# The routing of each mixture's first block moved into the stage ahead of it

## The reference

```
xn     = layernorm(x)
p      = softmax(xn @ router_W + router_b)        # 15 experts
cw     = p where p is among the 3 largest, else 0
x     += shared(xn) + sum over e of cw[e] * (relu(xn @ eW1[e] + eb1[e]) @ eW2[e] + eb2[e])
```

## Time and profile before

| | us |
|---|---|
| time, median of 3 runs | 2176.91 |
| lowest and highest | 2173.97, 2182.21 |
| the profiled execution's own time | 2175.81 |
| its span in the trace | 2174.1 |
| mean granted TensorE clock, as a share of full | 0.939 |

### The profile page before, as it was taken

How to read it: one execution, slowest core, us unless ns; L and a number is a source line. 1 busy time by engine, 2 the same in 40 slices (tenths; PEclk the granted TensorE clock), 3 DMA queues, 4 the chain that set the end, 5 groups by cost and what they waited for, 6 DMA issues and landing times. The chain is left out here.

```text
span 2174.1 us, 31063 instructions
## 1 busy us (share of the span) xinstructions
PE 1862.9 (86%) x9650; PEld 1279.9 (59%) x9650; DVE 1684.7 (77%) x4191; ACT 1200.8 (55%) x2004; POOL 903.4 (42%) x881
## 2 busy tenths in 40 slices
PE   6786699998899967674699978999999999988998
PEld 4564577777677723332577755555555555546777
DVE  6996788866788779998788867766766767738886
ACT  3442266653566634443466644665666666556666
POOL 1110255542455522220455544533533544325555
PEclk8998899999899987976799989999999999999999
DMA  3000344420444310000344400000000000004443
GB/s 101 6 5 5 129 147 147 147 73 1 147 152 157 132 40 1 1 0 0 125 155 160 147 0 1 1 1 1 1 1 1 1 1 1 1 1 166 166 168 126
DMA packets 87704, 142.28 MB, mean 65 GB/s; under 512 B 12369, under 2 KB 24337, under 8 KB 87026
## 3 DMA queue, kind: packets, MB, share of 16 engines
q1 hardware_dynamic: 85232, 139.50, 19.1%
q10 hardware_dynamic: 2306, 0.78, 0.2%
HBM read 136.38 MB, written 3.87 MB: 65 GB/s over the span
## 5 line engine op out<-in xcount | busy, mean ns | idle before, releaser
L2356 ACT ACTIVATE soft_prob<-psum 128x1024 f32<-128x1024 f32 (+3 forms) x384 | 302.6, 813 | 203.6 <-PE psum L2236 202.1
L2448 DVE TENSOR_REDUCE soft_mx<-psum 128x1 f32<-128x512 f32 (+2 forms) x352 | 230.8, 687 | 116.3 <-PE psum L2306 79.4
L2306 PE MATMUL psum<-soft_own,soft_stack 128*128 128x512 f32 (+3 forms) x768 | 249.3, 376 | 24.6 <-DVE soft_mx L2444 10.9
L2236 PE MATMUL psum<-soft_stack,soft_own 128*128 128x512 f32 (+3 forms) x768 | 225.3, 376 | 2.8 <-POOL soft_stack L2213 2.2
L2444 DVE CUSTOM_DVE_ANT_0 psum<-psum,s_soft_sel 128x384 f32<-128x384 f32 (+1 forms) x256 | 157.2, 638 | 64.9 <-PE psum L2306 64.1
L2236 PEld LDWEIGHTS psum<-soft_stack,soft_own 128*128 128x128 f32 x768 | 125.2, 189 | 133.1 <-issue 80.0
L2306 PEld LDWEIGHTS psum<-soft_own,soft_stack 128*128 128x128 f32 x768 | 139.8, 193 | 92.6 <-DVE soft_mx L2448 43.0
L2219 POOL TENSOR_SCALAR_AFFINE_SELECT soft_prob<-soft_prob 128x256 f32<-128x256 f32 x256 | 103.0, 409 | 203.6 <-ACT soft_prob L2356 200.7
L163 POOL TENSOR_TENSOR norm_rstd<-norm_mv,s_const_minus_half 128x4 f32<-128x4 f32 x64 | 65.3, 1020 | 272.8 <-DVE norm_mv L158 272.8
L2253 PE MATMUL psum<-soft_prob,soft_v_pad 128*32 128x512 f32 (+3 forms) x1536 | 163.6, 498 | 3.5 <-ACT soft_prob L2356 2.1
L941 POOL TENSOR_TENSOR ffn0a_low<-ffn0a_full,ffn0a_high 128x512 fp32r<-128x512 f32 x80 | 103.4, 1297 | 95.2 <-ACT ffn0a_high L1093 77.1
(11 more groups left out here) (443 smaller groups left out, 4930.1 us busy)
## 6 DMA issues: line engine op xcount, KB each, us to landing
ffn0a_cwb<-ffn0a_cw_dram SPq DMA_DIRECT2D x120, 256.0 KB, 6.5
ffn0b_cwb<-ffn0b_cw_dram SPq DMA_DIRECT2D x120, 256.0 KB, 6.2
ffn1a_cwb<-ffn1a_cw_dram SPq DMA_DIRECT2D x120, 256.0 KB, 6.5
ffn1b_cwb<-ffn1b_cw_dram SPq DMA_DIRECT2D x120, 256.0 KB, 6.2
s_ffn_w<-in_ffn_w SPq DMA_DIRECT2D x4, 1024.0 KB, 8.1
out_x<-x SPq DMA_DIRECT2D x8, 256.0 KB, 7.4
x<-in_x SPq DMA_DIRECT2D x4, 384.0 KB, 7.4
mamba_coef_dram<-mamba_out_coef SPq DMA_DIRECT2D x8, 96.0 KB, 1.6
```

What stands on the lines that cost most here:

```text
L2236: ins = pe.matmul(e_ps[:, n % 2, j, low(n):BLK], own[:, u % 3, 2 * pair + j, kt * P:(kt + 1) * P], stack[:, u % HT, qb * BLK + low(n):(qb ...
L2306: ins = pe.matmul(per_head[:, n, :], stack[:, u % HT, i * P:(i + 1) * P], own[:, u % 3, g, half * BLK:half * BLK + width], start=(n == 0), ...
L2356: nc.scalar.activation(prob[:, done % PROBS, :, low(n):BLK], e_ps[:, n % 2, :, low(n):BLK], ACT.Exp, scale=float(HD) ** -0.5).then_inc(exp ...
L2448: nc.vector.tensor_reduce(mx[:, i, half, heads.start:heads.stop], bank[:, 0:width * len(heads)].rearrange("p (g k) -> p g k", k=width), AX ...
```

## The change

The routing becomes a class `Routing`, used by a mixture for blocks 1 to 7 and by the stage ahead of it for the first block. The stage ahead stores the first block's `cwx` to DRAM as before, and `cwt` as well (`route_first`, 96x512), and ends when both have landed. In `mamba_output` the norm of the first block is done four blocks earlier (`AHEAD`), so that its routing can follow. In the linear stage shift and shares stand ahead of the add of block 6, largest and combine ahead of that of block 7, PE's transposes ahead of the last projection. In retention they stand between the last `invert` and the last `divide`, in the softmax stage they are new events of unit 13.

The mixture begins on SP with the 15 broadcast loads; then comes a load of `route_first` into the buffer `yt`, and in ffn0a the fetch. ACT waits for that load and copies it into `cwt`. The weight splits are cut anew: ACT does the first 4 experts of w1, 8 of w2, the rest of w1, and the rest of w2 behind the third expert; DVE does the low part of experts 0 to 3 ahead of its loop and that of 8 to 15 in it; POOL does experts 4 to 7. In block 0 the tokens, logits and routing of block 1 come three experts later (`late`).

The diff, cut to its core:

```diff
+class Routing:
...
+    def store(self, sp, q):
+        sp.wait_ge(self.cwx_ready, q - self.first + 1)
+        sp.dma_start(self.dram[q % 2, :, :], self.cwx[EXACT:EXACT + E, :]).then_inc(self.stored, 16)
+    def store_first(self, sp):
+        self.store(sp, 0)
+        sp.wait_ge(self.cwt_ready, 1)
+        sp.dma_start(self.first_dram[:, :], self.cwt[:, 0, :].bitcast(F32)).then_inc(self.stored, 16)
+        sp.wait_ge(self.stored, self.stored_after(0))
...
 # mamba_output
-        OUT_BANKS, AHEAD = 4, BLOCKS - 3
+        OUT_BANKS, AHEAD = 4, 1
...
+                if q == AHEAD + 3:
+                    route.shift(dve, 0)
+                if q == AHEAD + 4:
+                    route.probabilities(dve, 0)
+                    route.largest(dve, 0, ahead.pause)
+                    route.combine(dve, 0)
                 add(q)
...
 # ffn_stage, SP
             for q in range(BLOCKS):
                 spread(q)
+                if q == 0:
+                    sp.dma_start(yt[0:B2_ROWS, :], route.first_dram[:, :]).then_inc(first_loaded, 16)
+                if q == 0 and fetch is not None:
+                    for dst, src in fetch[0]:
+                        sp.dma_start(dst, src).then_inc(fetch[1], 16)
...
 # ffn_stage, POOL
+                    if split and g == 0 and e == 1:
+                        low_weights(w2_parts, w["w2"], (w2_high, 1), w2_pieces)
-                    if e == 3 and g + 1 < BLOCKS:
+                    if e == (6 if g == 0 else 3) and g + 1 < BLOCKS:
                         split_x(g + 1)
...
 # ffn_stage, PE
-            route(0)
             for n in range(EXPERTS):
                 g, e = divmod(n, NE)
+                late = 3 * (g == 0)
                 up(n)
-                if n == H_BANKS - 1:
-                    transpose_cw(0)
-                    tokens(1)
-                    route(1)
                 if n >= LAG:
                     down(n - LAG)
-                if e == 0 and 0 < g and g + 1 < more_blocks:
+                if e == late + (g == 0) and g + 1 < more_blocks:
                     tokens(g + 1)
...
-                if e == 8 and g + 1 < BLOCKS:
-                    transpose_cw(g + 1)
+                if e == 8 + late and g + 1 < BLOCKS:
+                    route.transpose(pe, g + 1)
...
 # ffn_stage, ACT
+            act.wait_ge(first_loaded, 16)
+            nc.scalar.copy(route.cwt[:, 0, :], yt[0:B2_ROWS, :]).then_inc(first_ready, 1)
             for n in range(EXPERTS):
                 parts_of(n)
+                if split and n == 2:
+                    high_weights(2, 1)
...
 # ffn_stage, DVE
             norm.resume(dve)
-            shift(0)
-            probabilities(0)
-            largest(0)
-            combine_weights(0)
+            norm.statistics(dve, 1)
+            if split:
+                low_weights(w1_parts, w["w1"], (w1_high, 1), w1_pieces, 0)
+                low_weights(w2_parts, w["w2"], (w2_high, 1), w2_pieces, 0)
...
                 if e - 1 in ON_VECTOR:
                     low_of(n - 1)
+                if split and n == 3:
+                    low_weights(w1_parts, w["w1"], (w1_high, 2), w1_pieces, 2)
+                if split and n == 5:
+                    low_weights(w2_parts, w["w2"], (w2_high, 2), w2_pieces, 2)
...
 # linear_attention_stage, DVE (the last round of its loop)
+                if not more:
+                    route.shift(dve, 0)
+                    route.probabilities(dve, 0)
                 add(q)
...
+                else:
+                    route.largest(dve, 0, norm.pause)
+                    route.combine(dve, 0)
                 add(q + 1)
...
 # retention_stage, DVE
                 invert(i)
+            route.pads(dve)
+            route.shift(dve, 0)
+            route.probabilities(dve, 0)
+            route.largest(dve, 0, norm.pause)
+            route.combine(dve, 0)
             divide(BLOCKS - 1)
...
 # softmax_events, unit 13
-            put((2, ("stat", BLOCKS)), (5, ("scale", BLOCKS)), (6, ("xt", BLOCKS)))
+            put((2, ("stat", BLOCKS)), (5, ("scale", BLOCKS)), (6, ("xt", BLOCKS)), (8, ("logits",)), (10, ("share",)),
+                (14, ("largest",)), (17, ("combine",)), (19, ("cwt",)), (22, ("copied",)))
```

More of the change, by code:

```diff
@@ L739, in mamba_output @@
         ahead = Prenorm(nc, const, x, name + "_a", xt_ps=banks.take(GT, P))
+        route = Routing(nc, const, route_weights, name + "_r", ps=banks.take(GT, P), first=0, stage=0,
+                        tiles=route_tiles(lambda n, shape, dt=F32: ctx.enter_context(nc.sbuf_tensor(f"{name}_{n}", shape, dt))))
         mixed = ctx.enter_context(nc.sbuf_tensor(f"{name}_mixed", [P, 2, HALVES, BLK], F32))
@@ L785, in _ @@
             ahead.copy(act, 0, 0)
+            route.exp(act, 0)
+            route.copy(act, 0)
         @block.tensor
@@ L812 @@
 LAG = 4
-B2_ROWS, EXACT = 96, 96
 PIECE, PIECES_KEPT = 1, 20
@@ L832, in pool_lows, with ffn_stage @@
     return n + 1 - vector_lows(n)
-def ffn_stage(nc, x, const, w, loaded, name, split=True, parts=None, out=None, fetch=None):
+def ffn_stage(nc, x, const, w, loaded, name, stage, split=True, parts=None, out=None, fetch=None):
     with ExitStack() as ctx:
@@ L847, in ffn_stage @@
         norm = Prenorm(nc, const, x, name + "_n", xt_ps=back_ps)
-        logit_ps = banks.take(GT, P)
-        cwt_ps = logit_ps
+        route = Routing(nc, const, w, name + "_r", ps=banks.take(GT, P), first=1, stage=stage,
+                        tiles=route_tiles(sb, 2))
         xt_parts = sb("xt_parts", [P, 2, 2, BLK], F32R)
@@ L1278, in linear_attention_stage @@
         norm = Prenorm(nc, const, x, name + "_n", xt_ps=banks.take(GT, P))
+        route = Routing(nc, const, router, name + "_r", ps=norm.xt_ps, first=0, stage=1, tiles=route_tiles(sb))
         q_ps = banks.take(BLK)
@@ L1313, in _ @@
                 bias(q - 1)
+        @block.sync
+        def _(sp):
+            route.store_first(sp)
         @block.tensor
@@ L1385, in _ @@
                     norm.transpose(pe, q + 4)
+                if not more:
+                    route.transpose(pe, 0)
                 project_out(q + 1)
@@ L1567, in retention_stage, with _ @@
         block = ctx.enter_context(nc.Block())
-        if fetch is not None:
-            @block.sync
-            def _(sp):
-                for dst, src in fetch[0]:
-                    sp.dma_start(dst, src).then_inc(fetch[1], 16)
+        @block.sync
+        def _(sp):
+            for dst, src in fetch[0]:
+                sp.dma_start(dst, src).then_inc(fetch[1], 16)
+            route.store_first(sp)
         @block.gpsimd
@@ L2385, in event @@
                     nc.scalar.copy(shift[:, :], ps[:, :, :]).then_inc(used, 1)
+                if kind == "share":
+                    route.exp(act, 0)
+                if kind == "cwt":
+                    route.copy(act, 0)
                 if kind == "oev":
@@ L2532, in hybrid_kernel @@
         weights = const_copies + mamba_copies
-        names = [n for n in const if n not in ("psum", "norm")] + list(mamba)
+        names = [n for n in const if n not in ("psum", "norm") and not n.startswith("route")] + list(mamba)
         early_names = ("ident", "minus_half", "in", "a_log", "conv_w", "conv_b")
```

405 lines of the change are left out of this document (239 added, 166 removed).

## The result

The changed kernel took 2208.3 us, median of 4 runs (2205.35 to 2210.54), against 2177.4 for the kernel before beside it. The ratio is 1.0139, with a 95% interval of 1.0115 to 1.0164: 31 us or 1.4% slower, and the interval lies clear of 1. The prediction had 2193 and a range of 2177 to 2201. The sign was right, the size is about twice what was forecast, and the time lies above the range.

The account below looks back on a forecast made before the run. PE was busy 86% and DVE 77%, but a mixture's head was taken as a chain, not a full engine. 2175.81 plus 14.9 us in the stages ahead and 1.9 in the mixtures gave 2192.6, stated as 2193; range 2177 to 2201.

Parts of the forecast that it names:

- The gate: ACT's first relu in a mixture, after the last transfer, about S+15.5; S is the start of its six DVE memsets.
- Rival A: Mixtures' heads: the first block's table doesn't wait for the 15 loads, first relu at S+11.8, total 2178; chance 0.13.
- The heads: Starts of the four mixtures: -2.8 in ffn0a, +0.8 ffn0b, +1.7 ffn1a, +2.2 ffn1b, together +1.9 us (-6 to +7).
- the gate's own moves: Shift of ACT's first relu against before: -4.8 us in ffn0a, +1.2 ffn0b, -0.7 ffn1a, -0.2 ffn1b.
- the net of -0.4 or 0 for block 1: Behind the first relu: added PE work against a shorter combine wait, -0.4 us in ffn0a and ffn0b, 0 in ffn1a and ffn1b.
- +2.4 for the low parts: ffn0a, ffn1a, ffn1b: two 1024-wide low parts inside DVE's loop can't use the wait for loads, +2.4 us each.
- Mamba's +6.7: Mamba's output: routing behind mix(7) on a gapless DVE, plus PE transposes, copies and stores at the end, +6.7 us (5.5 to 8).
- Softmax's +2.5: Softmax stage: logits and transposes on a busy PE, DVE's 4.4 us delaying PE by about 1, +2.5 us (0 to 4.5).
- Linear attention: End of the linear stage: routing on DVE stands ahead of and between the last two adds, +5.0 us (4.5 to 5.7).
- retention: Retention's end: routing and memsets (4.4 us) just overfill DVE's 4.03 us wait before its last division, +0.7 us (0.3 to 1.5).
- Rival C: Mixtures: DVE and POOL contention (+6) and block 1's later combine making DVE wait for its loads, total 2203; chance 0.14.
- Rival B: Mixtures: block 1's later routing ends PE's wait for its combine weights, 2 to 3 us a stage, total 2183; chance 0.15.

## Why the prediction was wrong

- The gate was right, in mechanism and size: forecast S+15.5, measured S+15.3 to S+16.0 in four heads, and moving one DMA took 39 us away. Rival A fell; its test, the table landing before the 12th load, was not met.
- The heads came to +10.8 in sum instead of +1.9, and the gate's own moves are not why (-3.4 in sum, forecast -4.5). Behind the gate the prediction had +2.0, -0.4, +2.4 and +2.4 for ffn0a, ffn0b, ffn1a and ffn1b; it came to 5.3, 0.3, 4.3 and 4.4. So the step that failed is the tally behind the gate in the three mixtures that split weights: the net of -0.4 or 0 for block 1, and +2.4 for the low parts as if they cost DVE's time alone. It let the later routing only shorten PE's wait for block 1. In the trace that wait is still 2.2 to 2.3 us, the low part puts a new one ahead of it (0.8 to 1.6 us, for the tokens), and PE's clock falls to 0.79 to 0.82 in that stretch, in ffn0a not in every profile. The lower clock right behind the gate is not the difference, since the kernel before has it too.
- Taking the low parts out of the loop gave back 1.8, 2.2 and 3.3 us, on average the +2.4 that they were given. What it leaves behind the gate, by the same count, is 3.0, -0.2, 1.4 and 1.1, where the net had -0.4, -0.4, 0 and 0: that part failed most in ffn0a. No run takes what is left apart.
- Mamba's +6.7 failed in the step "Mix(5) waits for PE's block 3, now behind the norm's transposes", taken at 0.9. It waited 2.2 us there and 3.4 at the last add, for PE's blocks took up to 3.62 us at the lower clock and not 2.05. With PE's pieces behind blocks that don't wait, the price is 5.9. Of the profile's +11.2, 2.1 lie ahead of the change (DVE's last instruction of the scan starts at 205.89 before, at 208.00 after, and at 205.5 to 206.9 in other runs of the same code).
- Softmax's +2.5 failed in "what waits for it there delays PE by about 1 more". I counted DVE's 4.4 us by duration and didn't look at what POOL does in those steps, though the prediction names that contention for the mixtures. That contention cost 3 to 4.5 us.
- Linear attention (+4.8 for +5.0) and retention (+0.6 for +0.7) were right; their chains were laid out row by row.
- Rival C had the contention, and no load waited at the start of block 1. Rival B's wait did not go in the changed kernel: 2.2 to 2.3 us are left in each mixture, less than before in ffn0a and ffn0b, and slightly more in the others.

## What to carry to other kernels

Before work is moved ahead of a stage, follow its result to the first reader: a small transfer queued behind large ones can gate a whole stage, and here moving one DMA took the kernel from 1.4% slower to 0.4% faster. A wait put in front of an engine is not over when it ends; behind waits of 7.6 us (ffn1b's gate) and 2.76 (softmax) PE ran the next 5 to 6 us at half rate, while behind one of 2.2 in ffn0b it kept its clock. So a new wait of PE can cost more than its length, and the granted clock behind it is to be looked at, in the kernel before as well. Moved DVE work with two SBUF inputs is to be checked against what POOL does at that time, not against DVE's idle share.

## What the runs showed of the hardware

- A DVE instruction of 0.21 us stood 2.77 us beside a POOL instruction of 3.60, until that one ended; with two table entries moved it took 0.21. The whole instruction is blocked, not slowed in proportion. The Trainium skill ("SBUF — State Buffer", section "Who interferes with whom") says so of a DVE instruction with two SBUF inputs; this trace agrees.
- In ffn1b the same 196 KB landed in 2.5 us at the head of SP's queue, in 3.9 from ACT's queue when issued with the first of the loads, and in 7.1 behind all fifteen on SP's, with the loads the same each time. Queue and time of issue are not told apart.
- PE's granted clock went from 1.00 to 0.50 after it had stood still for 2.76 us in the softmax stage, and was back at 1.00 from 1908 us on (1908 to 1918). Behind a wait of 2.2 us in ffn0b it stayed at 1.00 (585.94 to 593.94).
